# A four-layer graph network in one kernel: layer 2 with row-max scores on two row blocks, scores by head with a 32x32-block mask, and closed accumulations

## What is computed

```python
qkv = h @ W                                          # W is 128 x 384
q, k, v = split into 4 heads of 32 columns
mask = where(adj == 0, -inf, 0)
scores = einsum('bhid,bhjd->bhij', q, k) / sqrt(32) + mask
out = einsum('bhij,bhjd->bhid', softmax(scores, -1), v)
x = layernorm(x + out)
```

## Time and profile before

| | |
|---|---|
| median of three runs | 1164.12 us |
| profiled execution: span | 1163.7 us (no time of its own is listed beside the span) |
| busy: PE, DVE, ACT, POOL | 1002.3, 727.6, 450.3, 198.0 us |
| DMA queue of the DMAs that SP issues | 39.61 MB, 13.9% of 16 engines |
| mean granted TensorE clock | 0.933 |
| layer 2, first to last instruction | 499.4 to 983.0 us |

### The profile page before, as it was taken

How to read it: one execution, slowest core, us unless ns; L and a number is a source line. 1 busy time by engine, 2 the same in 40 slices (tenths; PEclk the granted TensorE clock), 3 DMA queues, 4 the chain that set the end, 5 groups by cost and what they waited for, 6 DMA issues and landing times. The chain is left out here.

```text
span 1163.7 us, 19102 instructions
## 1 busy us (share of the span) xinstructions
PE 1002.3 (86%) x5486; PEld 681.5 (59%) x5532; DVE 727.6 (63%) x2226; ACT 450.3 (39%) x734; POOL 198.0 (17%) x266
## 2 busy tenths in 40 slices
PE   3969999999997697926899999999999995899995
PEld 2748999999997586413444444444444442566663
DVE  7853455554454565635667767777777642688885
ACT  2111121121120265710444444544544442577762
POOL 5000110111100000050011111111111001155554
PEclk7879999999998899955799999999999998899998
DMA  6000000000000000004222222222223200000001
GB/s 185 1 28 19 10 19 19 10 18 18 9 0 1 9 0 0 0 8 108 55 56 55 54 54 54 54 58 64 66 60 68 66 1 3 1 27 27 27 27 37
DMA packets 32629, 40.07 MB, mean 34 GB/s; under 512 B 6352, under 2 KB 15696, under 8 KB 32592
## 3 DMA queue, kind: packets, MB, share of 16 engines
q1 hardware_dynamic: 32592, 39.61, 13.9%
HBM read 5.91 MB, written 4.19 MB: 9 GB/s over the span
## 5 line engine op out<-in xcount | busy, mean ns | idle before, releaser
L1221 DVE CUSTOM_DVE_ANT_0 junk<-bank,mask_ij 128x512 bf16<-128x512 f32 x256 | 170.7, 689 | 80.7 <-PE bank L1306 75.6
L1160 ACT ACTIVATE prob<-wide 128x1024 f32<-128x1024 f32 x128 | 128.0, 1024 | 44.5 <-PE wide L1320 44.1
L1306 PE MATMUL bank<-qk_st 96*128 96x512 f32 x256 | 122.2, 517 | 25.3 <-DVE mx L1221 15.8
L1319 PE MATMUL wide<-qk_st 128*128 128x512 f32 x256 | 116.2, 523 | 0.3 <-ACT prob L1160 0.3
L596 ACT CAST yT<-wide 128x512 fp32r<-128x512 f32 x48 | 28.1, 586 | 217.6 <-PE wide L699 162.7
L505 POOL TENSOR_SCALAR n_rstd<-n_aggr 128x4 f32<-128x4 f32 x64 | 12.6, 198 | 506.7 <-DVE n_aggr L498 494.6
L1306 PEld LDWEIGHTS bank<-qk_st 96*128 96x128 f32 x256 | 49.2, 201 | 82.5 <-DVE mx L1221 37.4
L1320 PE MATMUL wide<-mask_ji,identb 128*128 128x512 bf16 x226 | 88.8, 393 | 0.0
L58 PE MATMUL bank<-z,L3T_hi 128*128 128x256 f32 x256 | 73.8, 288 | 6.3 <-DVE z L657 6.3
L1633 PEld LDWEIGHTS bank<-Wh,pr 128*128 128x128 f32 x512 | 61.1, 196 | 23.8 <-issue 19.9
L1633 PE MATMUL bank<-Wh,pr 128*128 128x129 f32 x512 | 65.3, 282 | 10.9 <-ACT pr L1501 10.9
(11 more groups left out here) (256 smaller groups left out, 2273.3 us busy)
## 6 DMA issues: line engine op xcount, KB each, us to landing
qk_st<-qkT SPq DMA_DIRECT2D x192, 128.0 KB, 2.4
Xf<-X SPq DMA_DIRECT2D x16, 256.0 KB, 2.3
out_dram<-rc SPq DMA_DIRECT2D x16, 256.0 KB, 2.3
A<-in_adj_dram SPq DMA_DIRECT2D x1, 1024.0 KB, 5.5
w<-in_L_gnn_W_dram SPq DMA_DIRECT2D x2, 128.0 KB, 2.3
qk_st<-neg_row SPq DMA_DIRECT2D x16, 8.0 KB, 1.8
W<-in_L_gnn_W_dram SPq DMA_DIRECT2D x1, 192.0 KB, 2.4
w_sb<-in_L_gnn_w_dram SPq DMA_DIRECT2D x1, 64.0 KB, 5.0
```

Source lines behind the costliest of these rows:

```text
L1160: act.activation(flat(prob[jp][h][:]), wide[k % 2][:], ACT.Exp, scale=SCALE).then_inc(t_exp, 1)
L1221: dve.tensor_tensor_reduce(out=junk[k % 2][:], in0=src[:], in1=m.mask_ij[:, k % NT], scale=1.0, scalar=3.0 * MASKED, op0=ALU.add, op1=ALU.max,
L1306: pe.matmul(out[:], q_st[bp][0:3 * HD, h, i * P:i * P + P], k_st[bp][0:3 * HD, h], start=True, stop=True).then_inc(s_ps, 1)
L1319: pe.matmul(ps, k_st[bp][:, h, j * P:j * P + P], q_st[bp][:, h], start=True, stop=False)
```

## The change

Setup notes where `AhT` lies (`m.ah_at = nc.sbuf_base`); that tensor is not used after layer 1, and two of eight probability tiles are placed on it. In `layer2`:

- the two buffers of `qk_st` and of the high and low parts of xT become one; the probabilities, one buffer before, get two;
- each engine has its own order, and there are six stages; norm1's statistics, root and apply move to stage 1, the final norm's to stage 5;
- row-max scores take q high and k high straight from `qkT`, 32 rows per head, two heads per item on two row blocks into banks 4 and 5, and no longer wait for the stack; the maxima are turned in two halves (n and m) and negated by ACT while copying;
- scores_t go by head into banks 0 to 3; the mask is added afterwards by 16 matmuls of 32 x 32 blocks of the identity against `mask_q`, a rearranged copy of the mask that 16 DMAs make at the layer's start;
- denominators (D) and values (V) are separate accumulations in ring banks, each of four items;
- POOL takes over both norm applies, the low part of xT, the residual add and the copies back to `m.X`.

```diff
-        STAGE = dict(N=0, T=0, R=0, B=0, Y=1, x=1, q=1, k=1, v=2, s=2, g=3, n=3, t=3,
-                     a=4, e=4, o=4, d=4, m=4, r=4, b=4, y=4)
-        for what in ("s s g Y a n s N R x T a B s q k a s e s a s s t s t s d t m o r s t t s v b t s s y t t s s").split():
+        DEPTH = 6
+        STAGE = dict(N=0, T=0, R=0, B=1, x=1, q=1, k=1, v=2, s=2, n=2, m=3, t=3, E=3,
+                     D=4, V=4, e=4, f=4, d=4, o=4, c=4, b=5)
+        PE_ORDER = order("t s m D D s D D t s V V x s V V t s n s q d t o s k v T s")
+        ACT_ORDER = order("E E m e E E x f E E n q N E E k v")
+        DVE_ORDER = order("B s s s b s s s q c s k R s")
...
         @block.sync
+            for j in range(NT):
+                for c in range(4):
+                    sp.dma_start(mask_q[32 * j:32 * j + 32, c], m.mask_ji[32 * c:32 * c + 32, j]).then_inc(mask_in, 16)
...
+            def neg(b, p):
+                sp.wait_ge(n_row[p], after(b, 1))
+                sp.wait_ge(t_ps, after(b - 1, H, 2 * p + 2))
+                sp.dma_start(q_st[3 * HD:3 * HD + 1, 2 * p:2 * p + 2].bitcast(F32).rearrange("a h (t p) -> a (h t) p", p=P),
+                             neg_row[p][:].bitcast(F32)).then_inc(row_in[p], 16)
+            def stack(b, bp, h):
+                sp.wait_ge(t_ps, after(b - 1, H, h + 1))
...
...
+                if alive[3]:
+                    neg(s - 3, 1)
                 if alive[2]:
+                    b = s - 2
+                    sp.wait_ge(q_lo, after(b, 1))
+                    sp.wait_ge(k_lo, after(b, 1))
+                    stack(b, par, 0)
+                    stack(b, par, 1)
+                    neg(b, 0)
+                    stack(b, par, 2)
+                    stack(b, par, 3)
...
         @block.gpsimd
+                if alive[1]:
+                    norm1.root(pool, b + CREDIT, bp)
+                    norm1.apply(pool, b + CREDIT, bp, Xf[bp], lambda k: Xf[bp][:, k])
+                    pool.tensor_copy(batch_flat(m.X, b), flat(Xf[bp][:])).then_inc(x_f, 1)
+                    pool.wait_ge(x_c, after(b, 1))
+                    pool.tensor_tensor(xTr[1][:], xT[bp][:], xTr[0][:].bitcast(F32), ALU.subtract).then_inc(x_lo, 1)
+                if alive[5]:
+                    norm.root(pool, b + CREDIT, bp)
+                    norm.apply(pool, b + CREDIT, bp, r, lambda k: r[:, k])
+                    pool.tensor_copy(batch_flat(m.X, b), flat(r[:])).then_inc(x_b, 1)
                 if alive[4]:
+                    pool.tensor_tensor(flat(r[:]), flat(r[:]), batch_flat(m.X, b), ALU.add).then_inc(o_r, 1)
...
         @block.tensor
                     elif what == "s":
-                        pe.matmul(out[:], q_st[bp][0:3 * HD, h, i * P:i * P + P], k_st[bp][0:3 * HD, h],
-                                  start=True, stop=True).then_inc(s_ps, 1)
+                        pair, i = divmod(k, NT)
+                        pe.wait_ge(s_mx, after(b, TILES, 2 * k))
+                        for hh in range(2):
+                            c = slice((2 * pair + hh) * HD, (2 * pair + hh + 1) * HD)
+                            pe.matmul(bank[4 + hh][:], qkT[bp][c, Q_HI, i * P:i * P + P], qkT[bp][c, K_HI],
+                                      start=True, stop=True).then_inc(s_ps, 1)
                     elif what == "t":
-                        for jj in range(2):
-                            pe.matmul(ps, k_st[bp][:, h, j * P:j * P + P], q_st[bp][:, h], start=True, stop=False)
-                            last = pe.matmul(ps, m.identb[:], m.mask_ji[:, j], start=False, stop=True)
+                        for j in range(NT):
+                            if j % 2 == 0:
+                                pe.wait_ge(t_exp, after(b, EXPS, 2 * k - 1 + j // 2))
+                            pe.matmul(bank[j][:], k_st[:, k, j * P:j * P + P], q_st[:, k], start=True, stop=True)
+                        for c in range(4):
+                            for j in range(NT):
+                                q = slice(32 * j, 32 * j + 32)
+                                last = pe.matmul(bank[j][32 * c:32 * c + 32, :], m.identb[q, q], mask_q[q, c],
+                                                 start=False, stop=True, skip_group_check=True)
                         last.then_inc(t_ps, 1)
-                        for ps, stat in ((psO, None), (psD, ones)):
+                    elif what in "DV":
+                        acc = ring[what, 0]
                         for h in range(H):
+                            last = pe.matmul(acc[c, :], ones[:] if what == "D" else v[bp][:, k, c], prob[bp][h][:, k],
+                                             start=(k == 0), stop=(k == NT - 1), skip_group_check=True)
```

More of the change, by code:

```diff
@@ L1121, in _, with turned_max @@
+            pairs(pool, B, DEPTH, step)
         @block.scalar
         def _(act):
-            for s in (bn, x_hi, x_c, q_hi, k_hi, v_c, n_row, o_c, d_c):
+            for s in (bn, x_hi, x_c, q_hi, k_hi, v_c, n_row[0], n_row[1], o_c, d_c):
                 act.sem_inc(s, CREDIT)
-            act.sem_inc(t_exp, CREDIT * PAIRS)
+            act.sem_inc(t_exp, CREDIT * EXPS)
+            def turned_max(b, p, src):
+                act.wait_ge(n_ps[p], after(b, 1))
+                act.wait_ge(row_in[p], after(b - 1, 16))
+                act.activation(neg_row[p][:], src[0:2 * NT, 0:P], ACT.Copy, scale=-1.0).then_inc(n_row[p], 1)
@@ L1127, in step @@
             def step(s, par, alive, nth):
-                for what, k in ORDER:
+                for what, k in ACT_ORDER:
                     if not alive[STAGE[what]]:
@@ L1179, in _ @@
             norm1.credit_dve(dve)
-            norm1.credit_apply(dve)
             norm.credit_dve(dve)
-            norm.credit_apply(dve)
+            dve.wait_ge(w_in, 16)
+            split(dve, Wr[0][:], Wr[1][:], W[:, 0:2 * D], w_hi, 1, w_lo)
             def step(s, par, alive, nth):
-                for what, k in ORDER:
+                for what, k in DVE_ORDER:
                     if not alive[STAGE[what]]:
@@ L1188, in step @@
                     src = ring.get((what, k))
[L1189 to L1192, removed]
+                    b, bp = of_batch(what, s, par)
                     if what == "R":
@@ L1321, in step @@
[L1321 to L1334 removed]
+                        if isinstance(s, int) and s == STAGE["t"] and k == 0:
+                            pe.wait_ge(mask_in, 16 * 16)
@@ new lines, in step @@
+                        last.then_inc(t_ps, 1)
+                    elif what in "DV":
+                        acc = ring[what, 0]
+                        if what == "D" and k == 0:
+                            pe.wait_ge(t_exp, after(b, EXPS))
+                        if what == "V" and k == 0:
+                            pe.wait_ge(v_c, after(b, 1))
+                        for h in range(H):
+                            c = slice(h * HD, (h + 1) * HD)
+                            last = pe.matmul(acc[c, :], ones[:] if what == "D" else v[bp][:, k, c], prob[bp][h][:, k],
+                                             start=(k == 0), stop=(k == NT - 1), skip_group_check=True)
+                        last.then_inc(dn if what == "D" else av, 1)
@@ L1344, in step @@
                         last.then_inc(d_ps, 1)
-            pairs(pe, B, 5, step)
+            pairs(pe, B, DEPTH, step)
 def layer3(nc, m, ins, bank, out):
```

260 lines of the change are left out of this document (123 added, 137 removed).

## The result

The changed kernel takes **1135.42 us** (median of 6 runs, 1127.26 to 1137.61) against 1164.59 us for the kernel before (6 runs): ratio 0.9739, interval 0.9710 to 0.9768, 29 us faster. The forecast was 1130 in a range of 1103 to 1163.

What follows compares the result with a forecast made beforehand. The prediction took PE's own order to set layer 2's step, with 2.4 us of waits. Steps -25, fill -5, -3 and -4, drain +3 sum to -34 us: 1130 us, range 1103 to 1163 (its own range 1118 to 1143).

Steps and rivals of the forecast that it cites:

- steps -25: Layer 2's fourteen steps with scores and values: each 1.8 us shorter, from 26.94 to 25.15 us, -25 us.
- fill -12: Layer 2's start: no stack wait -5, memsets less work given to POOL -3, steps 2 and 3 at low clock -4.
- drain +3: Layer 2's end: POOL's add, apply and copy (1.3 + 3.2 + 0.6) replace DVE's 1.8 us, +3 us.
- Masks: Scores_t on PE: 16 small mask matmuls per head take 0.7 us, so t is 1.65 per head, -0.8 us per step.
- rival A: Scores_t on PE: 16 masks share one pass, handovers prompt; step 24.0 us, time 1114; chance 0.17.
- Pair and switches: Row-max scores on PE: two members overlap, 0.45 us per pair with a switch in and out, -1.2 us per step.
- The walk: One step followed item by item on PE and DVE: 22.5 us work, 2.7 waits, before s6 and T among them; 25.15.
- Rival D: Clock falls in the 1.5 us gaps before s6; a step's 22.5 us PE work doubles, four such make 1210; chance 0.03.
- one of its own signs of being wrong: Forecast wrong if the clock falls, small mask starts come 40 ns or more apart, or PE waits for POOL or DMA.
- POOL and SP: Per step: POOL's 12.5 us of about 25 stays hidden, and SP's stack DMAs land in time, so single buffers cost nothing.
- B: PE tiles: masks share across rows only (1.13 us per head), or row-max pairs run in series; step 26.5, 1149; chance 0.20.
- C: PE bound by issuing: masks 1.9 us per head give 1184, without sharing about 1265; decides from 44 ns each; chance 0.12.

Runs made afterwards that it cites:

- the same tiles in the old order: Kernel before, with the mask of two key tiles added by eight 32x32 matmuls per item instead of two full ones: 1175.24 us, ratio 1.0100.
- the filled wait: Kernel after, with the small transpose n of the first half of the row maxima done ten times instead of once: 1124.69 us, ratio 0.9654.
- q first: Kernel after, with q moved ahead of the sixth row-max pair in PE's order: 1119.71 us, ratio 0.9609.
- two waits mended: Kernel after, with q ahead of the sixth row-max pair, and transpose T and DVE's residual R behind the eighth pair: 1107.62 us, ratio 0.9527.
- B later: Kernel with two waits mended, and DVE's statistics B moved behind the first row-max pair: 1107.55 us, ratio 0.9510.
- the pair twice: Kernel after, with both matmuls of every row-max pair issued twice into the same banks: 1177.03 us, ratio 1.0114.

## Why the prediction was right, and where it was not

- **The sum: right, with luck.** Forecast -34: steps -25, fill -12, drain +3. The profile has -27.4, -10.8 and +3.1 for the same three, but it is the quickest execution; the one of 1138.27 us has -22.3, -7.4 and +3.1. The forecast of 1130 lies between the profiled execution (1127.3) and the median (1135.4). Two errors of opposite sign meet in it: masks priced too high, and a clock that was to stay at 1.00. In the fill, too, the forecast kept steps 2 and 3 at the low clock, and step 3 ran at 0.91.
- **Masks: mis-sized.** I priced a head's masks at 0.7 with switches; they cost 0.57 (1.50 less 0.93), the shared pass of rival A. That one term is worth 0.13 x 3.2 x 14 = 6 us. The full masks were priced too low as well: beside them a t takes 2.01 us and not 1.84, so a head saves 0.51 us where the forecast had 0.2.
- **Pair and switches: right.** 0.45 forecast, 0.43 found; twice the pair costs 8 x 0.23 more and single scores 0.42 each. The 0.2 us that the forecast put on every tiled stretch speaks against the change and holds; it sinks the same tiles in the old order. What the pairs brought over the 96-row scores no run shows by itself.
- **The walk: right.** s6 and T wait as forecast (1.5 and 0.9 forecast, 1.38 and 0.58 found). With masks at the 0.57 that they cost it gives 25.15 - 0.13 x 3.2 = 24.7; the full-clock step is 24.65. Rival A's 24.0 did not come: the masks share their pass, but with the switches it is not 0.43 us, and the waits stayed.
- **The clock: the step that failed.** Rival D had the right place, the wait before s6, but 0.03 of chance, and the forecast ran all steps at 1.00; that the clock falls was one of its own signs of being wrong. D's price was wrong too: it doubled the work of a whole step, some 20 us for each of four steps, and a fall costs 1.5 us. In fact four of twelve steps of the quickest execution lose 1.5 us each, and the filled wait shows it: 11 us of the median. That is why the median is 5 us above the forecast although the masks are cheaper.
- **POOL and SP: hidden, as forecast** (POOL 12.5 us per step, DVE 15.6), and in the twelve steps PE waits for neither. What I did not draw from it is that the move itself gains nothing.
- **Rivals B and C fell**: the two members of a pair and the 16 tiles of four row blocks share their pass (0.43 us long for 16), and C, which needed small starts 44 ns apart, has them at 3 ns.

Not settled: which waits bring a fall. With q first, alone or with the applies on DVE, with two waits mended and with B later the longest wait is 0.7 us, and none of the twelve steps holds one. But the kernel before waits 0.81 to 1.01 us without one, single 32-row scores wait 0.74 to 0.97 with one in each step, and the pair twice has falls in all its steps where the kernel after, with the same wait and less PE work, has them in a third. No run separates the wait from the rows that the matmuls around it use.

## What to carry to other kernels

Small tiles of the array were almost free in number here and dear in switches: 16 matmuls of 32x32 cost one pass, each entry and exit 0.1 us, so gather enough of them into one stretch before cutting a full matmul up. When PE waits in every step, look at what clock the next microseconds have, not at the wait alone; work that is already due is the best filling (here -16 us by moving one item), and even useless work paid (-11 us). Taking work off DVE, which sits idle a third of the step, brought next to nothing; ask first whether the engine sets the step.

## What the runs showed of the hardware

- Nine useless 128-column transposes per step made the kernel faster, 1124.69 us for 1135.42: the granted clock stayed at 1.00 (2.4 GHz) in all twelve steps, where it had fallen to 0.50 (1.2 GHz) for a stretch in four.
- Work on 32 rows went with more falls than work on 96 rows around like waits: every step of the kernel with single 32-row scores (waits of 0.74 to 0.97 us, mean clock 0.93), none of the kernel before (0.81 to 1.01 us, 1.00).
- Two executions of one program differ by 8.6 us in layer 2 (448.5 and 457.1). The twelve steps are alike, 301.4 us with four falls in both; 3.4 us of it lie in the fill (clock 0.66 against 0.90 in its last 22 to 25 us) and 5.1 behind the twelve steps (0.89 against 0.95).
- Sixteen 32x32 matmuls start some 3 ns apart and share one pass; a full or 96-row matmul right behind a tiled stretch takes 0.34 us to the next start instead of 0.23.
